# Where the sum over local attention's weights is taken: from one VectorE reduction per tile to an accumulator of ScalarE's exponentials

## The reference

```python
def _L0_attn_ref(x, ...):             # the local attention
    q = (x @ Wq.T + bq).reshape(B, S, 16, 32)
    k = (x @ Wk.T + bk).reshape(B, S, 4, 32)
    v = (x @ Wv.T + bv).reshape(B, S, 4, 32)
    q, k = rope(rmsnorm(q)), rope(rmsnorm(k))       # k and v repeated for 4 query heads each
    scores = einsum('bhqd,bhkd->bhqk', q, k) * scale
    mask = (key > query) | (abs(query - key) > 64)
    attn = softmax(where(mask, -10000, scores))
    return (attn @ v) @ Wo.T + bo

def _L0_ffn_ref(x, W_gate, W_qkv):    # the routed attention
    # per token the gate picks one of 16 heads' key and value; 16 query heads, causal softmax over 1024 keys
x = x + _L0_attn_ref(xn, ...) + _L0_ffn_ref(xn, ...)
```

## Time and profile before

| | |
|---|---|
| median of 3 runs | 674.92 us (674.49 to 675.19) |
| the profiled execution | 676.8 us, of which 675.6 us lie between the first and the last instruction (the span) |
| busy share of the span | PE 95%, DVE 68%, POOL 66%, ACT 54% |
| L1265, the sum over a tile's weights | 16 times, 1743 ns each |
| L1490, the exponentials | 256 times, 392 ns each (they overlap) |
| L1418, the exponential with an accumulator output | 16 times, each with a second instruction ACTIVATION_READ_ACCUMULATOR |

### The profile page before, as it was taken

The page is one execution under the profiler, slowest core; times in us unless marked ns, Lnnn a source line. Parts: engine busy times, 40 slices in busy tenths (PEclk is TensorE's granted clock), DMA queues, the critical chain, the costliest instruction groups (busy, mean ns, idle before and its releaser), DMA issues.

```text
span 675.6 us, 19434 instructions
## 1 busy us (share of the span) xinstructions
PE 641.0 (95%) x7432; PEld 509.3 (75%) x7432; DVE 459.9 (68%) x1296; ACT 362.5 (54%) x906; POOL 444.0 (66%) x384
## 2 busy tenths in 40 slices
PE   3888999999999999999999899999999999999997
PEld 2667788888788887888788677777777777777775
DVE  3847657658567665756665389887878787879454
ACT  4446554526453445445256555656565566656684
POOL 3856875386755649472896357776878687868730
PEclk9998999999999999999999899999999999999999
DMA  8623213231322142212216631502214131402011
GB/s 299 209 58 107 57 48 114 76 93 56 91 69 79 35 118 89 75 54 76 64 33 161 165 96 57 136 26 80 82 51 112 51 110 36 104 28 88 4 34 33
DMA packets 64942, 56.63 MB, mean 84 GB/s; under 512 B 6480, under 2 KB 48848, under 8 KB 64848
## 3 DMA queue, kind: packets, MB, share of 16 engines
q1 hardware_dynamic: 62704, 54.45, 27.2%
q10 hardware_dynamic: 2144, 0.93, 0.5%
HBM read 37.20 MB, written 17.89 MB: 82 GB/s over the span
## 4 chain that ended last, share of the span: by engine, by line
PE 86%; DVE 4%; POOL 3%; DMA 2%; issue 2%; ACT 2%; ACTq 1%; DVEq 0%; POOLq 0%
PE gemm L942 20%; PE s_ps L1051 12%; PE od_ps L1100 11%; PE st_ps L1084 10%; PE gemm L1028 7%; PE gemm L938 6%; PE od_ps L1114 5%; PE win L1002 4%; PE win L987 3%; PE s_ps L1123 2%; PE av L1014 2%; DMA rope_t<-rope 2%; PE av L1041 1%; PE tp L953 1%; PE tp L909 1%
## 5 line engine op out<-in xcount | busy, mean ns | idle before, releaser
L942 PE MATMUL gemm<-w_tok,xt 128*128 128x512 f32 (+1 forms) x768 | 185.9, 383 | 1.8 <-ACT xt L1410 0.8
L942 PEld LDWEIGHTS gemm<-w_tok,xt 128*128 128x128 f32 x768 | 131.1, 194 | 25.1 <-issue 1.2
L1317 DVE CUSTOM_DVE_ANT_0 s_ps<-s_ps,x_ln 128x512 f32<-128x512 f32 (+3 forms) x224 | 127.3, 618 | 25.1 <-PE s_ps L1051 24.8
L1051 PE MATMUL s_ps<-k_stack,w_tok 96*128 96x512 f32 (+2 forms) x336 | 101.2, 384 | 0.3 <-DVE x_res L1282 0.3
L1084 PE MATMUL st_ps<-w_tok,k_stack 98*128 98x512 f32 x288 | 99.2, 413 | 0.2 <-ACT p_loc L1538 0.2
L1538 ACT ACTIVATE p_loc<-st_ps 128x512 f32<-128x512 f32 x144 | 77.7, 598 | 36.1 <-PE st_ps L1084 35.0
L1490 ACT ACTIVATE p_loc<-win,l_max 128x96 f32<-128x96 f32 x256 | 61.1, 392 | 32.6 <-DVE l_max L1256 32.6
L1051 PEld LDWEIGHTS s_ps<-k_stack,w_tok 96*128 96x128 f32 x336 | 55.1, 188 | 27.8 <-DVE picked_fk L1317 12.3
L1659 POOL TENSOR_TENSOR p_loc<-p_loc,l_rec 128x1536 f32<-128x1536 f32 x16 | 44.1, 2759 | 36.6 <-DVE l_rec L1268 36.6
L1635 POOL TENSOR_TENSOR rope_b<-qkv,sin_t 128x128 f32<-128x128 f32 (+1 forms) x32 | 27.4, 878 | 62.0 <-DVE qkv L1234 61.8
L1538 ACT ACTIVATE p_loc_t<-st_ps 128x512 f32<-128x512 f32 x96 | 52.4, 599 | 19.4 <-PE st_ps L1084 18.9
(11 more groups left out here) (171 smaller groups left out, 1264.1 us busy)
## 6 DMA issues: line engine op xcount, KB each, us to landing
w_tok<-q_parts SPq DMA_DIRECT2D x72, 128.0 KB, 2.6
q_parts<-qt SPq DMA_DIRECT2D x120, 64.0 KB
x_ln<-x SPq DMA_DIRECT2D x8, 512.0 KB, 4.6
x_res<-x SPq DMA_DIRECT2D x16, 256.0 KB, 2.8
partial<-x_res SPq DMA_DIRECT2D x16, 256.0 KB, 2.3
w_tok<-partial SPq DMA_DIRECT2D x8, 512.0 KB, 5.1
raw<-w_tok SPq DMA_DIRECT2D x3, 1024.0 KB, 13.7
v_win<-v_rows SPq DMA_DIRECT2D x64, 48.0 KB, 2.2
```

Of the source, the lines that this page charges most:

```text
L942: i = e.matmul(g[:, 0:cols], xs[l][:, k, a * P:(a + 1) * P], w_tok_p[r][:, k, c0:c0 + cols], start=first, stop=last)
L1051: e.matmul(s_ps[bank][:, 0:cols], q_op[b][0:HALVES, i, h, :], k_stack[0:HALVES, b * S + c0:b * S + c0 + cols], start=True, stop=True).then ...
L1317: e.tensor_tensor_reduce(out=s[:, 0:cols], in0=s[:, 0:cols], in1=causal[:, S - width + c0:S - width + c0 + cols], scale=1.0, scalar=dst if ...
```

## The change

ScalarE's exponentials of the local attention get an accumulator output, so that each also gives the sum over its 96 keys, straight into one column of `l_sum`. VectorE's reduction over the tile is left out, with the wait for it. The reciprocal stands where it stood and now waits for the exponentials alone.

```diff
                 lane.wait_ge(*M["p_exp"].of((m, a, HKV - 1)))
                 if m:
                     lane.wait_ge(*M["p_r"].of((m - 1, a)))
-                e.tensor_reduce(l_sum[:, a, :], p_loc[a][:, :, :, :].rearrange("p g s k -> p (g s) k"), AX.X,
-                                ALU.add).then_inc(*M["l_sum"].did((m, a)))
-                lane.wait_ge(*M["l_sum"].of((m, a)))
                 e.reciprocal(l_rec[:, a, :], l_sum[:, a, :]).then_inc(*M["l_rec"].did((m, a)))
...
                         i = e.activation(p_loc[a][:, g, quad, :], win[:, g, quad * KEYS:(quad + 1) * KEYS], ACT.Exp,
-                                         bias=l_max[:, a, n:n + 1])
+                                         bias=l_max[:, a, n:n + 1], accum_out=l_sum[:, a, n:n + 1])
                     i.then_inc(*M["p_exp"].did((m, a, g)))
```

## The result

The changed kernel takes 678.39 us (median of 7 executions, 678.05 to 679.84) against 674.92 us before. The ratio is 1.0054 with a 95% interval of 1.0037 to 1.0070, so it is slower by 2.5 to 4.7 us; the forecast was +4.5. The profiled execution took 678.27 us, its span is 677.0 us.

A forecast was written before the change was run, and what follows sets the result against it. TensorE (PE) was taken as the bound, busy 95% of the span, so only shifts of PE's start count. Losses 6.8 less gains 2.3 (3.0 less POOL's 0.7) give +4.5 on 674.92: 679.4 us, range 674.8 to 685.0.

The forecast's parts named there:

- tile 0, `gemm` bank: Bank VectorE frees after ScalarE's copy `qt` behind the exponentials: margin 0.78 us, PE 0.7 us late.
- tile 2, transposes: PE's transposes of the tile before need the bank of `win`: margin 0.51 of 1.48 us, 1.0 us late.
- tile 6, transposes: PE's transposes of the tile before need the bank of `win`: margin 0.84 us, 0.6 us late.
- tiles 4, 5, 9, 11, transposes: Same wait of PE's transposes for the bank of `win` at four more tiles: 1.2 us late in all.
- tile 8, bank and transposes: `gemm` bank freed after ScalarE's `qt`, margin 0.26 us: PE 1.2 us late, the tile's late transposes included.
- tile 14: ScalarE's `v_all` late, so VectorE's `picked_fv` and the last transposes' copy too: PE's `values` 1.1 us late.
- tile 15: `qt` and four copies right behind the exponentials, margin 0.45 us: PE's `values` 1.0 us late.
- three waits behind VectorE: PE idle behind VectorE's sum near 203.62, 254.85 and 326.54 us: 0.8, 0.8 and 1.4 us, together 3.0 us gained.
- POOL's cap: POOL's rotary step for the next tile gets later behind the exponentials, losing 0.3 and 0.4 us of the last two gains.
- free read: Rival: a read fits before the next bias fetch and costs ScalarE nothing, 3.0 us gained, 671.9 us; chance 0.09.
- waiting read: Rival: each read waits for its exponential, 0.187 us a read, 3.0 us a tile, 700 us; chance 0.07.
- softer margins: Rival: PE's loads run ahead and take back part of late starts, half the losses show, +1.1, 676.0 us; chance 0.13.

The follow-up runs named there:

- Neither: The kernel before without VectorE's reductions and without accumulator outputs, `l_sum` holding ones, so the local softmax lacks its division: 671.38 us, ratio 0.9940.
- three tiles: The kernel before with accumulator outputs at tiles 7, 9 and 12 alone, VectorE's reduction at the other 13: 672.03 us, ratio 0.9967.
- later reductions: The kernel before with VectorE's reduction and reciprocal of tiles 7, 9 and 12 later in its own list, no accumulator outputs: 672.18 us, ratio 0.9968.
- half dose: Against the kernel before, accumulator outputs for key heads 0 and 1 only, VectorE reducing heads 2 and 3: 673.94 us, ratio 0.9985.
- double dose: The changed kernel with a one-element ScalarE copy in front of each exponential: 703.82 us, ratio 1.0421 against the kernel before.
- two complements: Against the kernel before, accumulator outputs at tiles 7, 9 and 12 alone, and in another kernel at the other 13 alone: 672.03 and 681.76 us.

## Why the prediction was right

The path was the forecast's: the read is paid where PE stands right behind ScalarE, and the reduction is won back at three places. The sum of the sizes came out 1.0 above the medians (+4.5 against +3.5) and agrees with the profiles (+4.4), where one of the terms, tile 0, agrees by luck (below). Each term against the trace: the shift of the same matmul between the profiles before and after, from just ahead of the place to just behind it.

| term | forecast us | measured us |
|---|---|---|
| tile 0, `gemm` bank | 0.7 | 0.7 |
| tile 2, transposes | 1.0 | 0.9 |
| tile 6, transposes | 0.6 | 0.5 |
| tiles 4, 5, 9, 11, transposes | 0.5, 0.25, 0.2, 0.25 | 0.4, 0.2, 0.1, 0.1 |
| tile 8, bank and transposes | 1.2 | 1.25 |
| tile 14 | 1.1 | 1.1 |
| tile 15 | 1.0 | 1.2 |
| three waits behind VectorE | -3.0 | -0.7, -0.9, -1.3 |
| POOL's cap, twice | 0.7 (0.3, 0.4) | 0.54, 0.33 |
| net | +4.5 | +4.4 |

The net shift is from -0.98 before tile 0's place to +3.41 behind tile 15's; of tile 0's 0.7, 0.2 were taken back by 60 us, and small shifts elsewhere added 0.3. The medians differ by 3.5, with 2.5 to 4.7 in the interval, so the missing 0.9 need not be real. A part of it is: the forecast let the second stage only start later, but at 533 us PE's loads wait 0.35 us less than before (first before, then after).

```profile
532.73 0.20 PEld L1123 LDWEIGHTS s_ps<-idt,rope_sq 128*128 128x128 f32 x2 [0.60 <-issue]
...
534.13 0.20 PEld L1123 LDWEIGHTS s_ps<-idt,rope_sq 128*128 128x128 f32 x2 [0.25 <-issue]
```

The shift falls there from 1.75 to 1.40. It does so in the profile of every kernel that has fewer than the 16 reductions, and in none of those that have all 16 or 16 half ones. Why is open.

- **The price of a read.** Starts of two exponentials lie 0.315 apart, of which the read took 0.093; a run took 5.26 us, 1.44 more. The free read and the waiting read are both out. The value came from a pair whose exponential had 16 elements and no bias, and it held for 96 elements with a bias.
- **The reduction was on the path three times in 16.** "Neither" shows its size, 3 us or a little less; three tiles and the later reductions show that it lies at these tiles.
- **Tile 0's term agrees by luck.** Its margin of 0.78 was read in an execution in which low clock had made PE late there. In the second profile of the kernel before the margin is nothing, and the term would have been 1.5 instead of 0.7. That the table has 0.7 on both sides rests on the low clock standing at this place in both first profiles.
- **Losses are 1.48 less the margin, and add up.** Shown by the half dose (-0.6 where 1.7 was in proportion), the double dose, and the sum of the two complements. The softer margins are out.
- **ScalarE not full, and yet waited for.** It was busy for 48% of the stretch, and the price was paid in ten places where it was at work for PE at the moment.
- **The cap by POOL** was real and a little larger: 0.9 instead of 0.7.
- **What was wrong:** PE's idle time between 60 and 350 us was to grow by 1.7.

```profile
60.00:350.00 290.00, 284.10 (x2482) 237.52 (x2483) 167.53 (x373) 153.79 (x637) 187.53 (x143) 1.00 0.25 75
```

It is 5.9 us against 6.4 in the earlier trace rows. PE did less in that time (2482 matmuls against 2490) and yet counts as busy for longer, while the time of its loads fell by 2.5 us, from 240.0 to 237.5. The waits for ScalarE's exponentials are 6.1 us in 16 places on the row of the loads and 1.6 in 4 on that of the matmuls: the records of neighbouring matmuls overlap, so a late start of some tenths disappears in them. The sum of PE's idle time was the wrong thing to name. VectorE was to be 28 us less busy; its busy time fell by 23.5. ScalarE's busy share was also to grow by 48 us by lengths: the reads were 243 ns long in these runs instead of 190, 62 us, but they overlap with the exponentials, and ScalarE's busy time rose by 20.4.

## What to carry to other kernels

Work moved from one engine to a less busy one is priced at the places where someone stands right behind it: take the added time, subtract the margin of each consumer, sum what is left, and set against it only the idle time that the removed work had caused. Where the removed work is on the path in three of sixteen rounds, do the change in those three, or move the work within its own engine's list; both beat the whole change here, 672.0 and 672.2 against 678.4. A less busy engine says nothing: half a dose lost less at its margins than it gained and was 0.6 us faster, the full one was 3.5 slower. And read a margin in more than one profile: tile 0's was 0.78 us in one execution and nothing in the next, because TensorE's clock had been low at different times.

## What the runs showed of the hardware

An accumulator output is a second instruction on ScalarE for each ACTIVATE. Its record is 0.19 to 0.30 us long, and it takes 0.093 us of the engine, the same behind 16 and behind 96 elements; a copy of one element took as much.

```profile
377.69 3.80 PE L1028 MATMUL gemm<-w_o,attn_t 128*128 128x512 f32 x9 [1.53 <-DVE attn_t L1273]
```

The same idle time stands in every one of these profiles, and the clock fell behind it in two. So idle time of PE was there each time before the clock fell, and yet it mostly did not fall; what decides is not shown here.
